# Tail and front of an attention kernel: a pair's block copies on two queues, one transpose ahead of a mask, the last row in two column halves, and one read between casts

## What is computed

```python
q = heads(x @ Wq + bq)
k = heads(x @ Wk + bk)
v = heads(x @ Wv + bv)
scores = jnp.einsum('bhqd,bhkd->bhqk', q, k) * scale
scores = jnp.where(mask[:, None] == 0, -jnp.inf, scores)
attn = jax.nn.softmax(scores, axis=-1)
out = jnp.einsum('bhqk,bhkd->bhqd', attn, v)
out = out.transpose(0, 2, 1, 3).reshape(b, s, D_MODEL)
...
x = _layernorm(x + (out @ Wo + bo), axis=-1)
```

## Time and profile before

| | us |
|---|---|
| median of 3 runs | 808.75 |
| lowest and highest run | 808.1, 809.65 |
| the profiled execution | 808.37 |
| its span | 806.6 |
| busy in the span: PE, PE weight loads | 799.6, 680.2 |
| busy in the span: DVE, ACT, POOL | 635.5, 267.5, 540.2 |

### The profile page before, as it was taken

One profiled execution on the slowest core, in us unless ns is written; L12 is line 12 of the kernel. 1 busy time (PEld: TensorE's weight loads), 2 busy tenths in 40 slices (PEclk: granted clock), 3 DMA queues, 4 the chain that ended last, 5 costly groups with the idle time before them and its releaser, 6 DMA issues.

```text
span 806.6 us, 26965 instructions
## 1 busy us (share of the span) xinstructions
PE 799.6 (99%) x11777; PEld 680.2 (84%) x11777; DVE 635.5 (79%) x1008; ACT 267.5 (33%) x349; POOL 540.2 (67%) x437
## 2 busy tenths in 40 slices
PE   9999999999999999999999999999999999999997
PEld 7888888888888888888888888888888888888876
DVE  5869777878778887778887787877878777876895
ACT  6642333322333222333223332223332333323223
POOL 0387668766678676776766767666866768755672
PEclk9999999999999999999999999999999999999999
DMA  9335435254453434534345344544525435234342
GB/s 330 127 81 173 116 113 179 84 150 130 120 177 98 147 109 119 176 114 134 117 115 171 123 132 119 156 130 119 164 81 171 125 106 178 71 108 120 94 110 103
DMA packets 65110, 106.64 MB, mean 132 GB/s; under 512 B 11744, under 2 KB 28640, under 8 KB 62944
## 3 DMA queue, kind: packets, MB, share of 16 engines
q1 hardware_dynamic: 52512, 87.85, 34.9%
q10 hardware_dynamic: 12480, 17.06, 8.2%
HBM read 54.53 MB, written 16.78 MB: 88 GB/s over the span
## 4 chain that ended last, share of the span: by engine, by line
PE 99%; DMA 0%; DVE 0%; issue 0%; POOLq 0%; POOL 0%
PE ring L373 16%; PE ring L374 15%; PE ring L375 15%; PE ring L525 7%; PE ring L526 7%; PE ring L529 7%; PE psum_s L476 6%; PE psum_s L446 6%; PE ring L467 6%; PE psum_s L480 6%; PE psum_s L478 6%; DMA x_raw<-in_xt 0%; PE ring L393 0%; PE ring L401 0%; PE ring L397 0%
## 5 line engine op out<-in xcount | busy, mean ns | idle before, releaser
L1186 POOL TENSOR_TENSOR soft<-soft,top 128x1024 f32<-128x1024 f32 x62 | 122.6, 1977 | 21.2 <-DVE top L973 21.2
L237 POOL TENSOR_TENSOR soft<-soft,inverse 128x1024 f32<-128x1024 f32 x62 | 118.8, 1917 | 26.0 <-DVE inverse L980 25.9
L977 DVE TENSOR_REDUCE total<-soft 128x16 f32<-128x1024 f32 x62 | 75.3, 1214 | 54.2 <-ACT soft L719 54.2
L719 ACT ACTIVATE soft<-soft 128x1024 f32<-128x1024 f32 x62 | 65.9, 1062 | 112.5 <-POOL soft L1186 112.5
L373 PE MATMUL ring<-x_hi,wk_hi 128*128 128x512 f32 x256 | 102.8, 401 | 0.0
L374 PE MATMUL ring<-x_lo,wk_hi 128*128 128x512 f32 x256 | 99.9, 390 | 0.0
L375 PE MATMUL ring<-x_hi,wk_lo 128*128 128x512 f32 x256 | 99.8, 390 | 0.0
L525 PE MATMUL ring<-wo_hi,ot_hi 128*128 128x512 f32 x252 | 99.2, 394 | 0.0
L526 PE MATMUL ring<-wo_lo,ot_hi 128*128 128x512 f32 x252 | 98.9, 393 | 0.0
L754 ACT CAST s_hi<-v 128x1024 fp32r<-128x1024 f32 x27 | 28.3, 1046 | 207.7 <-DVE v L909 207.7
L373 PE MATMUL ring<-x_hi,wq_hi 128*128 128x512 f32 x248 | 96.7, 390 | 0.0
(11 more groups left out here) (127 smaller groups left out, 1862.0 us busy)
## 6 DMA issues: line engine op xcount, KB each, us to landing
pt<-soft SPq DMA_DIRECT2D x248, 64.0 KB, 2.4
x_raw<-in_xt SPq DMA_DIRECT2D x15, 1024.0 KB, 6.8
row<-in_x SPq DMA_DIRECT2D x60, 256.0 KB, 2.7
out_rows<-row SPq DMA_DIRECT2D x60, 256.0 KB, 2.6
pt<-soft ACTq DMA_DIRECT2D x232, 64.0 KB, 2.4
v<-in_xt SPq DMA_DIRECT2D x27, 512.0 KB, 4.5
adj<-in_adj SPq DMA_DIRECT2D x16, 128.0 KB, 2.7
kt<-in_wk SPq DMA_DIRECT2D x4, 256.0 KB, 6.0
```

Of the source, the lines that this page charges most:

```text
L237: ops.tensor_tensor(soft_of(c), soft_of(c), on_keys(inverse[:, c % 2, :]), ALU.mult).then_inc(normed, 1)
L977: nc.vector.tensor_reduce(total[:, c % 2, :], by_row_head(soft_of(c)), AX_XY, ALU.add).then_inc(summed, 1)
L1186: nc.gpsimd.tensor_tensor(soft_of(c), soft_of(c), on_keys(top[:, c % 2, :]), ALU.subtract).then_inc(centred, 1)
```

## The change

There are four edits. `last_done` and `last_shifted` are semaphores.

1. `SHARED` becomes all tiles, so that T-4 and T-3 are placed by both queues like the others. ACT's list gets `place(T - 4)` after `exp(T - 3)` and `place(T - 3)` after `exp(T - 2)`, ahead of `read_ot(PAIRS - 3)`.
2. DVE's `turn(T - 3)` moves ahead of `mask(T - 2)`; it stood behind that mask and `add_y(T - 7)`.
3. For the last row the addition of epsilon to the variance moves from POOL to DVE. DVE normalises the row in two column halves, SP stores the first and ACT the second.
4. ACT's `read_k(3)` moves in between the second and the third `split_weight_sums`.

```diff
-SHARED = (*range(TILES - 4), TILES - 2, TILES - 1)
+SHARED = range(TILES)
...
@@ sync
-            for c in range(T - 8, T):
+            for c in range(T - 8, T - 1):
                 store(c)
-            for n in range(4):
+
+            sp.wait_ge(last_done, 1)
+            sp.dma_start(out_dram[T - 1, :, 0:HALF], row_of(T - 1)[:, 0:HALF]).then_inc(stored[3], DMA)
+            for n in range(3):
                 sp.wait_ge(stored[n], DMA * TILES // 4)
+            sp.wait_ge(stored[3], DMA * (TILES // 4 + 1))
...
@@ scalar
             read_k(2)
-            for n in range(4):
-                split_weight_sums(n)
+            split_weight_sums(0)
+            split_weight_sums(1)
             read_k(3)
+            split_weight_sums(2)
+            split_weight_sums(3)
...
             exp(T - 4)
             exp(T - 3)
+            place(T - 4)
             exp(T - 2)
+            place(T - 3)
             read_ot(PAIRS - 3)
             exp(T - 1)
...
             norm_by_act(T - 2)
+            act.wait_ge(last_done, 2)
+            act.dma_start(out_dram[T - 1, :, HALF:D], row_of(T - 1)[:, HALF:D]).then_inc(stored[3], DMA)
...
@@ vector, finish_last_row
-                norm_row(dve, nc.vector, c)
+                dve.wait_ge(row_moments, c + 1)
+                nc.vector.tensor_scalar(shifted[:, c % 8, :], moments[:, c % 8, 1:2], EPS, None,
+                                        ALU.add).then_inc(last_shifted, 1)
+                dve.wait_ge(row_rstd, c + 1)
+                for columns in HALVES:
+                    nc.vector.tensor_scalar(row_of(c)[:, columns], row_of(c)[:, columns], moments[:, c % 8, 0:1],
+                                            rstd[:, c % 8, :], ALU.subtract, ALU.mult).then_inc(last_done, 1)
...
@@ vector
             read_v(T - 5)
+            turn(T - 3)
 
             mask(T - 2)
             add_y(T - 7)
-            turn(T - 3)
             mask(T - 1)
...
@@ gpsimd, make_rstd
-                pool.wait_ge(row_moments, c + 1)
-                nc.gpsimd.tensor_tensor(shifted[:, c % 8, :], moments[:, c % 8, 1:2], eps,
-                                        ALU.add).then_inc(row_shifted, 1)
-                pool.wait_ge(row_shifted, c + 1)
+
+                if c < TILES - 1:
+                    pool.wait_ge(row_moments, c + 1)
+                    nc.gpsimd.tensor_tensor(shifted[:, c % 8, :], moments[:, c % 8, 1:2], eps,
+                                            ALU.add).then_inc(row_shifted, 1)
+                    pool.wait_ge(row_shifted, c + 1)
+                else:
+                    pool.wait_ge(last_shifted, 1)
```

More of the change, by code:

```diff
@@ L135, in attention_kernel @@
                                                         sem("row_done"))
-        row_shift, last_done = sem("row_shift"), sem("last_done")
+        row_shift, last_shifted, last_done = sem("row_shift"), sem("last_shifted"), sem("last_done")
         pe_went_on, dve_went_on, pool_went_on = sem("pe_went_on"), sem("dve_went_on"), sem("pool_went_on")
@@ L255, in norm_row @@
             eng.wait_ge(row_rstd, c + 1)
-            done = last_done if c == TILES - 1 else row_done
             ops.tensor_scalar(row_of(c), row_of(c), moments[:, c % 8, 0:1], rstd[:, c % 8, :],
-                              ALU.subtract, ALU.mult).then_inc(done, 1)
+                              ALU.subtract, ALU.mult).then_inc(row_done, 1)
         block = ctx.enter_context(nc.Block())
@@ L299, in store @@
             def store(c):
[L300 to L303, removed]
+                sp.wait_ge(row_done, c + 1)
                 sp.dma_start(out_dram[c], row_of(c)).then_inc(stored[c % 4], DMA)
```

## The result

The changed kernel takes 810.82 us (median of 21 runs, 809.21 to 812.83), the kernel before 808.88 beside it (21 runs). The ratio is 1.0025, interval 1.0016 to 1.0033: **slower by 1.9 us**. The forecast was +1.05, with "no change that can be told" at 0.82. The time, 810.82, lies inside the range (808.1 to 810.9); the sign of the sum was right, its size and the verdict were not.

The account below looks back on a forecast made before the run. PE was taken to bound the kernel, with 99% of the chain of waits. Front 0, tail +1.25 and end -0.2 sum to +1.05 us, giving 809.8 on the median of 808.75 (809.4 on the profiled execution); range 808.1 to 810.9.

Parts of the forecast that it names:

- no change that can be told: Verdict on the whole kernel: the sum lies inside the 0.2%, 1.6 us, that a measurement cannot tell; chance 0.82.
- What bounds the kernel: PE holds 99% of the chain of waits; the pair's copies land 6.5 us before the mix, so PE does not wait.
- The front edit: At the first score, ACT's earlier read removes PE's 0.21 us stand, but the gain is not kept: 0, bounds -0.21 and 0.
- The second reason: At row 0's output product, PE already waits for DVE's subtraction, so arriving 0.21 us earlier it waits 0.21 longer.
- The tail edits: Before row T-6, late exponential and ACT's copy issues delay the read and DVE's subtraction: PE +1.25 us, bounds 0 and +1.9.
- slack of 0.43: At row T-6, DVE's subtraction ended at 775.54, 0.43 us before PE's first matmul at 775.97.
- The step that failed: On ACT, T-3's four issues start with T-2's exponential at 772.0 + 0.16, take 2.65 us and end at about 774.8.
- rival B: T-3's issues on ACT are long (3.27 us), PE stands 1.9, the halved store gains nothing: 810.7 to 810.9; chance 0.12.
- A: Rival: the issues cost ACT little or the read slips in ahead, PE waits for nothing new: 808.55 us; chance 0.13.
- Rival C: The change does what it says, faster by over 1.6 us, at 807.0 or less; chance 0.02.
- The end edit: After PE's last matmul, epsilon on DVE and the last row stored in halves: -0.2 us, bounds +0.2 and -0.45.

Follow-up runs that it names:

- e6: The changed kernel with ACT's four copies of T-3 moved behind the read of mixed rows and the exponential of T-1: 809.32 us, ratio 1.0004.
- e1: The kernel before with the two tail edits alone (blocks of T-4 and T-3 on both queues, turning of T-3 ahead of T-2's mask): 811.02 us, ratio 1.0025.
- e2: The kernel before with only the split of the copies of T-4 and T-3 over both queues, the turning not moved: 809.64 us, ratio 1.0012.
- e3: The kernel before with only the turning of T-3 moved ahead of T-2's mask, SP issuing all copies of T-4 and T-3: 809.55 us, ratio 1.0014.
- e10: The kernel before with the end edit alone (epsilon on DVE, last row in halves, second store on ACT): 809.16 us, ratio 1.0004.
- e4: The changed kernel without its two tail edits, so the front and end edits alone: 808.75 us, ratio 1.0001.
- e12: The changed kernel once more, unaltered, a second look at one profiled execution: 810.89 us.
- e8: The changed kernel timed again, unaltered, on the same chip as other follow-up runs: 810.35 us, ratio 1.0021.
- e5: The changed kernel with seven unused matmuls of 128x512 on PE ahead of its wait for the late subtraction: 811.0 us, ratio 1.0031.
- e11: The changed kernel once more, unaltered, for one profiled execution: 813.29 us.
- g1: The changed kernel with PE's warm-up cut into 30 matmuls of 128 columns in place of 15 of 256: 814.55 us, ratio 1.0072.
- g2: The changed kernel with PE's warm-up cut into 60 matmuls of 64 columns in place of 15 of 256: 823.38 us, ratio 1.0186.
- e7: The changed kernel with all eight copies of T-3 issued by ACT and none by SP: 814.12 us, ratio 1.0064.
- e9: The changed kernel with all eight copies of T-3 on ACT and sixteen unused matmuls filling PE's wait: 814.57 us, ratio 1.0061.

## Why the prediction was right and wrong

**What bounds the kernel: right.** PE was the chain, nobody waited for the pair's blocks, and bringing them forward gained nothing: e6 sends T-3's copies later than after does and is faster.

**The front edit: the number 0 holds, the reasons don't.** In after the score starts 0.32 after the start of the projection's last matmul, so the 0.21 of the earlier trace rows is gone. But it is gone as well in e1, e2, e3 and e10, in which the read still stands behind all four casts. After, then e10:

```profile
30.03 0.39 PE L375 MATMUL ring<-x_hi,wk_lo 128*128 128x512 f32 x1
30.35 0.36 PE L446 MATMUL psum_s<-kt,qt 32*64 32x64 f32 x15
```
```profile
29.74 0.39 PE L375 MATMUL ring<-x_hi,wk_lo 128*128 128x512 f32 x1
30.06 0.69 PE L446 MATMUL psum_s<-kt,qt 32*64 32x64 f32 x39
```

PE stood for the read in the one profiled execution of before and in none of the fifteen others. So it is a matter of the execution, and no run shows what the edit is worth. The second reason, that PE would meet DVE's late subtraction and lose the gain again, did not hold either. DVE's subtraction now ends at 62.06 + 1.21 = 63.27 and the load for row 0's product starts at 63.33, right behind it as in the earlier trace rows; but from the first score to row 0 it is 33.09 before and 33.10 in after, so that chain moves along with the score.

**The tail edits: mechanism right.** Step by step: exponential at 772.0, measured 772.44; issues to 774.8, measured 774.94; reading at 774.9, measured 775.03; PE at 777.2, measured 777.36, with the whole execution some 0.4 later up to the mix. From row T-7 to row T-6 after loses 0.94 against the profile of before, where the forecast had 1.25, and 1.35 against e4 and e10. What sets before apart is the stop in its mix: the forecast took its slack of 0.43 from that profile, and in e4 and e10 the subtraction, which waits there for DVE's own list and not for the reading, ends less than 0.1 ahead of row T-6. For the executions of the lower group the forecast of +1.05 is what happened (809.4 forecast on the profiled execution, 809.73 measured; their median of 809.77 is 0.9 above that of before), in part by luck, since the stop was in the one profile and not in the other.

**The step that failed** is "They start with the exponential ... and end at about 772.2 + 2.65": one price for the four issues. The earlier trace rows had both prices, 3.27 and 2.65, and the forecast took the smaller as the likely one and gave the larger to rival B, at 0.12, with the argument that SP is done with T-3 by then. SP is not what matters: it issues nothing while T-3's copies go out of ACT, neither in after (2.44) nor in e12 (3.68). Either price comes up from one execution to the next: of the nine profiled executions with four copies ahead of the reading, four took 2.4 to 2.6 (after, e1, e2, e8) and five 3.1 to 3.7 (e5, e11, e12, g1, g2).

**A term that it put at nothing, without a reason,** is the clock: a wait of PE can cost more than its length. Of the waits at row T-6 those of 1.46 (after, e1) left the clock whole, and those of 2.0 (g2), 2.3 (g1), 2.54 (e11) and 4.02 (e7) brought it to half, at 1.4 to 1.6 us, while e12's 2.66 did not. The upper group is what a long wait with the low clock behind it adds up to: 1.1 more of waiting and 1.4 of clock on the 809.7 of the first profile make 812.2, amid its 811.7 to 812.8; e12, long but with the clock whole, is at 810.9, the upper edge of the lower group. That all ten executions of the upper group are of this kind is inferred. None of the ten was profiled, only e11, which lies above them (813.29) with a stop of PE of 0.59 at 679.85 in it. For it speak the mean clocks: 0.997 or 0.998 in all ten, 0.998 to 1.0 in the eleven of the lower group. Against it speaks one of e8's three long executions, 812.6 at 0.999. And e1, with the same tail, has the median of after, 811.02, without a low clock: four of its ten executions take 811.2 to 811.6 at 0.999 or 1.0, and the profiled one of them has a stop of PE of 1.06 at 680. So how much of the median's loss each of the three causes makes, long issues, low clock and stops, stays open; that the tail edits bring it is shown.

**The rivals.** A (the issues cost ACT little) was excluded by 1.54 us of "issue" ahead of the reading. B named what happens in part of the executions, issues of over three microseconds and a PE wait of 1.6 and more, but not the clock. That the median, 810.82, lies in its 810.7 to 810.9 is chance: it is the last time of the lower group. Rival C did not happen. And the verdict: with a sum of +1.05 against a threshold of 1.6, longer issues worth 1 us and a low clock worth 1.4 in part of the executions were enough to carry the median over it.

**The end edit: -0.2, measured -0.12.** Counted from the start of PE's last matmul, normalising starts 0.08 earlier (2.30 in place of 2.38), as forecast; the two halves take 0.73 in place of 0.55, so that the row is done 0.10 later; and the landing of the half is 1.8 in place of 2.0. The Trainium skill's slope (DMA: Bandwidth & Descriptors, Anatomy of one DMA — SWDGE (gpsimd) path), of which the forecast said that the rows did not bear it out, agrees with these landings: an estimate of 0.3 less for the half, 0.2 to 0.3 measured. Its constant, fitted for copies that GpSimd issues, does not: 2.0 plus the slope would be 2.6 for the 256 KB that landed in 2.0. Its other rule there (Issuing engines are not separate DMA queues), that a second issuer saves only sequencer time that is usually small, holds for the gain and not for the cost: here the second issuer's sequencer time, 0.61 a copy, stood ahead of a reading that PE needed.

## What to carry over

Before copies are put on an engine that also computes, look at what stands behind them in its list and how much slack that has, and count the issues at the long price as well as the short one. Where a later line can take them (behind the reading, as in e6), the same split costs little (0.15 in the profile of e6). Before slack is taken from a profile, look whether the engine had a stop in that stretch that other passes of the same work don't have. And a profile of one execution shows one of several ways in which a kernel runs: where a term has two prices in the trace, the forecast should be a mixture of both.

## What the runs showed of the hardware

- Issuing T-3's copies of 64 KB takes ACT 0.51 us for the first and 0.61 for each one behind it. The long one among them takes 1.25 (g2) to 1.85 (e12), each time beside a fetch of instructions.
- The granted clock fell behind waits of PE of 2.0, 2.3, 2.54 and 4.02 us, not behind those of 1.46 (after, e1) and, once, 2.66 (e12); the low stretch cost 1.4 to 1.6 us. With PE kept busy in the wait the mean clock was 0.998 or more in all fifteen executions (e5, e9), and without it 0.997 or less in all five of e7. The Trainium skill (TensorE: Matmul & The Clock Gate, Part 1) has the gate looking at TensorE's activity on a beat of its own, so that the same program can fall on either side; e11 and e12, of one kernel, are such a pair.
- PE stops now and then for 0.4 to 1.7 us with nothing to wait for in the profile ("issue"), and more than once at the same place: 0.38 in before and 1.70 in e8 in the mix of T-6, T-5; 0.59 in e11 and 1.06 in e1 at 680; 0.93 in e3 and 1.11 in e10 at 382. Such a stop can hide a wait that comes right behind it.
- The matmuls of the warm-up start 0.213 us apart with 256, 128 and 64 columns (after, g1, g2).
